# The instructions of a 64-tile attention kernel in new orders on all five engines

## The reference

```python
y   = clip(modulated_linear(x, style) + bias, -256, 256)
q   = l2norm(layernorm(y) @ Wq) * q_scale        # 16 heads of 64
k, v = y @ Wk, y @ Wv ; k = l2norm(k) * k_scale  # 2 null keys in front
x1  = x + softmax(8 * q @ k.T + alibi, causal) @ v @ Wout
kx  = modulated_linear(x1, style2)               # per token: 16 heads of 16
om  = modulated_linear(softmax(kx @ kx.T / 4) @ kx, style3)   # over the heads of one token
gates -> cluster, tile of 64 (argmax twice) ; comp = tanh(gelu(om @ w1) @ w2)
out = x1 + layernorm(om + mag(comp, tables[tile]) * directions[tile])
```

## Time and profile before

| | |
|---|---|
| time, median of 3 runs | 1833.0 us (1832.64 to 1834.09) |
| profiled execution | 1833.11 us |
| its span, first to last instruction | 1831.3 us |
| busy: PE, DVE, ACT, POOL | 94%, 84%, 65%, 64% |
| mean granted clock of PE | 0.97 |
| instructions | 62542 |

### The profile page before, as it was taken

The page is one execution under the profiler, slowest core; times in us unless marked ns, Lnnn a source line. Parts: engine busy times, 40 slices in busy tenths (PEclk is TensorE's granted clock), DMA queues, the critical chain, the costliest instruction groups (busy, mean ns, idle before and its releaser), DMA issues.

```text
span 1831.3 us, 62542 instructions
## 1 busy us (share of the span) xinstructions
PE 1718.0 (94%) x24806; PEld 1439.5 (79%) x24806; DVE 1545.9 (84%) x4182; ACT 1198.5 (65%) x2418; POOL 1173.0 (64%) x903
## 2 busy tenths in 40 slices
PE   4789999999999999999999999999999999999752
PEld 3568888888888888888888888888888888888641
DVE  5567799888989998889989988899899888998744
ACT  2456677777667777776676777676777777667431
POOL 0345557776777677767776777677767776776433
PEclk8899999999999999999999999999999999999875
DMA  4001222222222221222122212221222122212221
GB/s 150 15 9 29 42 49 49 49 55 59 48 46 53 59 49 45 53 59 49 45 56 56 52 42 55 56 52 45 55 54 55 43 52 55 55 47 50 55 54 44
DMA packets 341245, 93.63 MB, mean 51 GB/s; under 512 B 278289, under 2 KB 338097, under 8 KB 341169
## 3 DMA queue, kind: packets, MB, share of 16 engines
q1 hardware_dynamic: 338096, 82.04, 20.6%
q0 software_dynamic: 3072, 10.52, 2.1%
HBM read 58.95 MB, written 33.55 MB: 51 GB/s over the span
## 4 chain that ended last, share of the span: by engine, by line
PE 88%; DVE 5%; ACT 2%; POOL 1%; DMA 1%; issue 1%; SPq 1%; POOLq 0%; ACTq 0%; DVEq 0%
PE pa L442 29%; PE pb L421 7%; PE pa L449 6%; PE ps L645 6%; PE ps L487 6%; PE ps L472 5%; PE ps L479 4%; PE pc L542 4%; PE pc L622 3%; PE pa L421 3%; PE ps L557 3%; PE pb L433 3%; PE ps L489 2%; PE pb L551 2%; PE pb L428 2%; PE pc L568 1%
## 5 line engine op out<-in xcount | busy, mean ns | idle before, releaser
L1131 POOL TENSOR_TENSOR rn<-nrg,mhalf 128x16 f32<-128x16 f32 x64 | 186.6, 2915 | 160.6 <-DVE nrg L1037 160.6
L1117 POOL TENSOR_TENSOR rn<-nrg,mhalf 128x16 f32<-128x16 f32 x64 | 193.2, 3018 | 119.5 <-DVE nrg L970 119.4
L442 PE MATMUL pa<-wv,y 128*128 128x512 f32 x768 | 209.6, 409 | 0.0
L442 PE MATMUL pa<-wq,xnTs 128*128 128x512 f32 x768 | 205.1, 411 | 0.3 <-ACT kcat L703 0.3
L442 PE MATMUL pa<-wk,y 128*128 128x512 f32 x768 | 194.3, 402 | 0.9 <-ACT qn L722 0.9
L442 PEld LDWEIGHTS pa<-wq,xnTs 128*128 128x128 f32 x768 | 139.3, 191 | 51.8 <-issue 23.5
L442 PEld LDWEIGHTS pa<-wk,y 128*128 128x128 f32 x768 | 139.3, 188 | 30.9 <-ACT qn L722 1.7
L1111 POOL TENSOR_TENSOR pr<-pr,rden 128x1056 f32<-128x1056 f32 x64 | 124.7, 1949 | 54.5 <-DVE rden L943 51.8
L442 PEld LDWEIGHTS pa<-wv,y 128*128 128x128 f32 x768 | 135.4, 189 | 23.2
L1006 DVE TENSOR_TENSOR qn<-qn,rn 128x1024 f32<-128x1024 f32 x64 | 112.7, 1762 | 15.6 <-POOL rn L1117 15.0
L1092 POOL TENSOR_TENSOR kn<-kn,rn 128x1024 f32<-128x1024 f32 x64 | 122.0, 1905 | 5.0
(11 more groups left out here) (216 smaller groups left out, 4863.3 us busy)
## 6 DMA issues: line engine op xcount, KB each, us to landing
xT<-in_xT SPq DMA_DIRECT2D x64, 128.0 KB
x<-in_x SPq DMA_DIRECT2D x64, 128.0 KB, 2.1
kxdr<-kxn SPq DMA_DIRECT2D x64, 128.0 KB, 1.7
x1d<-x SPq DMA_DIRECT2D x64, 128.0 KB, 1.8
vm<-kxdr SPq DMA_DIRECT2D x128, 64.0 KB
odr<-o SPq DMA_DIRECT2D x256, 32.0 KB
on<-odr SPq DMA_DIRECT2D x64, 128.0 KB
xb<-x1d SPq DMA_DIRECT2D x64, 128.0 KB, 2.2
```

Source lines behind the costliest of these rows:

```text
L442: last = mm(bank, part(lhs(a_, k)), part(rhs(b_, k)), start=(n == 0), stop=(n == 3 * CK - 1))
L1117: g.tensor_tensor(rn[:, 0, :], nrg[:, 0, :], mhalf[:, :], ALU.pow).then_inc(S("q_rsqrt"), 1)
L1131: g.tensor_tensor(rn[:, 1, :], nrg[:, 1, :], mhalf[:, :], ALU.pow).then_inc(S("k_rsqrt"), 1)
```

## The change

The diff, cut to its core. SP:

```diff
-                if live(i, 6):
-                    sp.dma_start(plain(x1d, t6), x1[:, p, :]).then_inc(D("x1_out", p), 16)
+                if live(i, 5):
+                    wait(sp, "kxn_done", t5)
+                    sp.dma_start(plain(kxdr, t5), kxn[:, :]).then_inc(S("kx_out"), 16)
+                    wait(sp, "kx_out", t5, 16)
+                    for u in range(2):
...
                 if live(i, 11):
-                    wait_dma(sp, "x1_out", t11, 1 - p)
-                    sp.dma_start(xb[:, 1 - p, :], plain(x1d, t11)).then_inc(D("x1_back", 1 - p), 16)
+                    wait(sp, "res_done", t11)
+                    sp.dma_start(plain(out_t, t11), res[:, 1 - p, :]).then_inc(D("out", 1 - p), 16)
...
+                if live(i, 9):
+                    wait_dma(sp, "x1_out", t9, 1 - p)
+                    sp.dma_start(xb[:, 1 - p, :], plain(x1d, t9)).then_inc(D("x1_back", 1 - p), 16)
...
```

PE, DVE and POOL where the prediction speaks of them:

```diff
+                if live(i, 4):
+                    wait(pe, "xm2_done", t4)
+                    linear_T(two(pb, C), wk2, xm2).then_inc(S("kxT_mm"), 1)
...
+                if live(i, 1):
+                    wait(pe, "q1_raw", t1)
+                    project(pa[:, 1, :], lambda a, k: y3f[:, 1 - p, a, k, 0:P],
+                            lambda a, k: wk[:, a, k, 1 * 512:2 * 512])
...
+                if live(i, 3):
+                    wait(dve, "probs", t3)
+                    v.tensor_reduce(den[:, :], heads, AX, ALU.add).then_inc(S("den_done"), 1)
+                    wait(dve, "den_done", t3)
+                    v.reciprocal(rden[:, :], den[:, :]).then_inc(S("rden_done"), 1)
+                if live(i, 7) or live(i, 8):
+                    if live(i, 8):
+                        wait(dve, "local_exp", t8)
+                    route = links_from(0, t7)
                     route(v.tensor_scalar(fl[:, :, :], esc[:, :, :], 1.0, None, ALU.add))
                     route(v.reciprocal(fl[:, :, :], fl[:, :, :]))
                     route(v.scalar_tensor_tensor(out=over[:, :, :], in0=bc(both(fl), 2, KN), scalar=float(KN - 1),
                                                  in1=bc(CO["steps"], 1, 2 * NC), op0=ALU.mult, op1=ALU.subtract))
+                if live(i, 4):
+                    wait(dve, "x1T", t4)
+                    modulate(xm2, two(pb, 0), sty[:, 1, :, :], t4).then_inc(S("xm2_done"), 1)
...
+                if live(i, 3):
+                    wait(pool, "rden_done", t3)
+                    g.tensor_tensor(heads, heads, bc(rden[:, :], 2, J), ALU.mult).then_inc(S("pr_norm"), 1)
...
+                if live(i, 9):
+                    wait_dma(pool, "x1_back", t9, 1 - p)
+                    g.tensor_tensor(xb[:, 1 - p, :], xb[:, 1 - p, :], gb[:, 1, :], ALU.add)
```

More of the change, by code:

```diff
@@ L512, in step @@
[L512 to L536, removed]
+                if live(i, 7):
+                    if 1 - p == 1:
+                        nc.tensor.transpose(pb[:, C:C + P], hidn[:, :, :].rearrange("p u h -> p (u h)"), ident[:, :])\
+                            .then_inc(S("hT_mm"), 2)
@@ L545, in step @@
                     last.then_inc(S("mix_scores"), 1)
[L546 to L553, removed]
-                if live(i, 4):
[L555 to L559, removed]
+                if 1 - p == 1:
+                    if live(i, 7):
+                        wait(pe, "gelu_done", t7)
+                if live(i, 4):
+                    wait(pe, "x1_done", t4)
+                    to_T(two(pb, 0), x1[:, p, :]).then_inc(S("x1T"), 1)
+                if live(i, 2):
+                    wait(pe, "v1_done", t2)
+                    four(pa[:, 1, :], qn, 4).then_inc(S("qT1_mm"), 1)
                 if live(i, 1):
@@ L581, in step @@
+                if live(i, 3):
+                    wait(pe, "pT_done", t3)
+                if live(i, 4):
+                    wait(pe, "kxn_done", t4)
+                if live(i, 6):
+                    wait_dma(pe, "on2_in", t6, p)
+                    to_T(two(pb, 0), on2[:, p, :]).then_inc(S("omT"), 1)
+                if live(i, 3):
                     for r in range(HP):
                         for t, s in ((0, 0), (1, 1), (1, 0), (0, 1)):
-                            last = pv_tile(r, t, s, p)
+                            last = pv_tile(r, t, s, 1 - p)
@@ new lines, in step @@
+                if live(i, 5):
+                    for g in range(QG):
+                        last = fn(kbd[:, g, :], pc[:, 0:2 * P], ACT.Identity, bias=0.0, scale=pick4[:, g:g + 1])
+                    last.then_inc(S("mask_done"), 1)
+                if live(i, 3):
+                    wait(act, "pr_sub", t3)
+                    fn(pr[:, :, :, :], pr[:, :, :, :], ACT.Exp).then_inc(S("probs"), 1)
+                if live(i, 7):
+                    if 1 - p == 1 and live(i, 9):
+                        wait(act, "comp_mm", t9)
+                    if 1 - p == 1:
+                        wait(act, "hT_mm", t7)
+                    if 1 - p == 1:
+                        fn(hT[:, :], pb[:, C:C + P], ACT.Gelu, bias=b1[:, :]).then_inc(S("gelu_done"), 2)
@@ new lines, in step @@
+                if live(i, 7):
+                    if 1 - p == 1:
+                        wait(act, "comp_mm", t7)
+                    if 1 - p == 1:
+                        for o in range(2):
+                            last = fn(comp[:, :, o], pb[:, C + P:C + P + 4].rearrange("p (u o) -> p o u", o=2)[:, o, :], ACT.Tanh,
+                                      bias=b2[:, o:o + 1])
+                        last.then_inc(S("comp_done"), 2)
+                if live(i, 3):
+                    wait(act, "pv_mm", t3)
@@ new lines, in step @@
+                if live(i, 8):
+                    wait(dve, "scores_done", t8)
+                    v.tensor_tensor(own[:, :, :], sc[:, p, :].rearrange("p (c k) -> p c k", k=TPC),
+                                    bc(chosen[:, p, 0, :], 2, TPC), ALU.mult).then_inc(S("own_done"), 1)
+                    wait(dve, "own_done", t8)
+                    v.tensor_reduce(lsc[:, :], own[:, :, :].rearrange("p c k -> p k c"), AX, ALU.add)\
+                        .then_inc(S("local_score"), 1)
+                if live(i, 7):
+                    wait(dve, "zT_mm", t7)
+                    modulate(zd, two(pb, C), dem[:, 2, :, :], t7).then_inc(S("z_dem"), 1)
+                    wait(dve, "z_dem", t7)
+                    v.tensor_tensor(zT[:, :, :], zd[:, :, :, :].rearrange("p k b l -> p k (b l)"),
+                                    bc(cols[:, OB, :], 2, P), ALU.add).then_inc(S("zT_done"), 1)
@@ L895, in step @@
+                if live(i, 3):
+                    wait(dve, "sim_mm", t3)
                     v.tensor_tensor(by_slot(pr)[:, :, 0:R7, :], ps[:, 0:2, 0:R7 * J].rearrange("p t (r j) -> p t r j", j=J),
@@ L1022, in step @@
-                if live(i, 5):
-                    wait(dve, "x1T", t5)
-                    modulate(xm2, two(pb, 0), sty[:, 1, :, :], t5).then_inc(S("xm2_done"), 1)
-                if live(i, 6):
-                    wait(dve, "mix_exp", t6)
-                    v.tensor_reduce(sm2[:, :], A2[:, :, :], AX, ALU.add).then_inc(S("mix_sum"), 1)
-                    wait(dve, "mix_sum", t6)
-                    v.reciprocal(sm2[:, :], sm2[:, :]).then_inc(S("mix_rsum"), 1)
-                    wait(dve, "mix_rsum", t6)
-                    v.tensor_tensor(A2[:, :, :], A2[:, :, :], bc(sm2[:, :], 2, H), ALU.mult).then_inc(S("a_done"), 1)
```

662 lines of the change are left out of this document (315 added, 347 removed).

## The result

| | before | after |
|---|---|---|
| time, median (4 runs each) | 1833.0 us (1832.6 to 1834.1) | 1845.2 us (1844.1 to 1845.4) |
| ratio, 95% interval | | 1.0064 (1.0047 to 1.0082) |
| span of the profiled execution | 1831.3 us | 1842.3 us |
| period, 53 steps (tile 9's q projection to tile 62's) | 26.11 us | 26.90 us |

What follows compares the result with a forecast made beforehand. PE bounded the kernel before (26.08 us a step); after, a PE and DVE loop of 26.4 would. 1833.1 less 34 at the ends plus 17 in steady steps gives 1816 us, range 1797 to 1845.

Steps and rivals of the forecast that it cites:

- The ends: Filling and emptying of the pipeline, tail included: 34 us gained together, bounds 20 and 40.
- The 2.4 us that I added for dropped waits: Fill: followed loss of 19.6 us taken as 22, against 33.5 before, for a gain of 11.5.
- The tail: After the last score matmul to the kernel's end: 28 us, against 30.4 before.
- The gain of the emptying: From step 64 to the end, tail included: loss 63 instead of 86.9 us, gain 24, taken as 22.5.
- my 3 us for dropped waits: Emptying: 3 us added to a followed PE loss of 32, making 35 instead of 62.3.
- the routing block: Steady step: DVE's routing instruction, 0.29 us, held 1.6 beside POOL's pr_norm, in front of xm2.
- The loop: Steady step: PE kx linear to omT, DVE om to rden, routing, xm2; 26.4 us, 0.3 longer than PE's step.
- DVE's term: DVE's part of the steady cycle, from om to rden: 16.6 us.
- the steady term, +17: Steady steps: 0.3 us lost in each of 58 steps, 17 us in all.
- rival 2: Steady step: gamma's hold 0.6 and table load 0.25 also count; a good half real, 0.8 a step, 1845 us; chance 0.28.
- Rival 1: Steady step: no stall, only 0.05 us a step lost; 1802 us (1794 to 1808); chance 0.23.
- rival 3: Ends gain only 20 us and steady steps cost 20; 1833 us; chance 0.07.

Runs made afterwards that it cites:

- run 3: Changed kernel with DVE's routing part 0 to 2 moved behind the copy pn, and yn moved behind the two y-low subtractions: 1807.1 us.
- run 1: Changed kernel with DVE's routing part 0 to 2 moved from in front of xm2 to behind the copy pn: 1808.6 us.
- run 6: Changed kernel, every order kept, with POOL's pr_norm made to wait for the third routing instruction: 1805.2 us.
- run 11: Changed kernel with yn moved behind the two y-low subtractions and ScalarE's Gelu replaced by Identity: 1814.4 us.
- run 2: Changed kernel with yn moved behind the two y-low subtractions, so POOL's gamma multiply cannot get between them: 1824.5 us.
- run 7: Changed kernel with ScalarE's Gelu replaced by Identity, so table loads fall from 67 to 3: 1831.7 us.
- run 4: Changed kernel with POOL's addition of beta moved from the step's end to the next step, in front of gamma: 1847.2 us.
- run 9: Changed kernel with routing behind pn, yn behind the y-low subtractions, and the exp table loaded early on every second step: 1802.7 us.

## Why the prediction was wrong

**The ends were about right.** The first k projection started at 54.39 and took 3.05 (57.4 for 57.9); the kn transposes began at 66.22, for 66.35; steps 2 and 3 of the fill ended at 75.51 and 96.54, for 75.6 and 96.5:

```profile
54.39 3.05 PE L441 MATMUL pa<-wk,y 128*128 128x512 f32 x12
66.22 1.06 PE L448 MATMUL pa<-ident,kn 128*128 128x128 f32 x8 [1.62 <-POOL kn L1123]
75.51 3.16 PE L441 MATMUL pa<-wv,y 128*128 128x512 f32 x12
96.54 1.67 PE L441 MATMUL pa<-wv,y 128*128 128x512 f32 x6
```

The 2.4 us that I added for dropped waits were not there (gain 13.9 for 11.5). The tail behind the last score matmul is 28.1 us (1842.3 less 1814.2) for 28. The gain of the emptying is 5 us less than I took: steps 65, 66 and 67 took 22.9, 21.9 and 17.1, not 20.4, 17.5 and 14.5, and my 3 us for dropped waits cover only a part of that. In 65 and 66 PE waits 1.11 and 2.10 for xm2, because the routing block is in the emptying too, and I had priced it in steady steps alone; in run 3 PE waits 0.51 for it in step 66 (last line):

```profile
1736.97 1.16 PE L420 MATMUL pb<-xm,wk 128*128 128x128 f32 x8 [1.11 <-DVE xm L880]
1758.12 1.16 PE L420 MATMUL pb<-xm,wk 128*128 128x128 f32 x8 [2.10 <-DVE xm L880]
1813.07 1.11 PE L657 MATMUL pb<-wsc,zT 128*128 128x136 f32 x4
1720.13 1.16 PE L420 MATMUL pb<-xm,wk 128*128 128x128 f32 x8 [0.51 <-DVE xm L880]
```

From tile 62's q projection to the end it is 155.3 us in the changed kernel, and 150.6 in run 3; between tile 63's and the end 128.8 and 125.2. How much of that is the block is not shown: in run 1, without the block, the latter is 128.8 too. What else made the three steps longer stays open.

**The loop was the right one**, and its terms can be read off one turn, om 1018.40 to om 1045.20: DVE from om to rden's end 17.14 (forecast 16.6); routing and xm2 2.76 (2.92); kx linear to om 6.90 (6.9). Sum 26.80, 26.98 in the next turn, for 26.4. L988 took 1.83 for 1.9, and run 6 shows its hold as the cause. The 0.5 that is missing is DVE's term: 17.14 holds gamma's 0.53 and the 0.22 for the q squares; without them it is 16.39, 0.2 under my figure. In the next turn the q squares are in time, but res holds L951 (0.59, not 0.18), which I had not named. So my 26.4 is itself too long: 16.39 + 2.76 + 6.90 is 26.05 (an estimate from this one turn), no more than PE's own step. That run 11 comes out at 26.34, and its time at 1814.4, so near to my 1816, is in part luck, since gamma's hold on L909 fills the difference.

**The step that failed** is the steady term, +17: in "I take 26.4 and 58 steps" the loop's DVE part leaves out gamma's hold and the wait for the exp table, which stand in rival 2 alone. The steady steps lost 42.0 us, 26.90 a step. Rival 2 had the same loop with "0.6 + 0.25" on top and "a good half real, 0.8 a step: 1845"; the period rose by 0.79, to the 26.9 that I had named as its sign, and the time is 1845.2. That it meets the time to 0.2 us is luck: its 46 us in the steady steps were 42, and its 34 at the ends 31. Runs 2 and 7 price its terms at 0.34 and 0.23 a step, 0.57 together, and run 11 without them is at 26.34. I had both terms from the rows, in a loop that I had found to be closed already; I gave them to a rival because PE before had absorbed such holds. That argument didn't apply: before, PE was the bound and DVE waited 1.39 a step for it. In the closed loop a hold on DVE's half has no such wait to go into; one beside PE's half has (run 4). Rival 1 (no stall) fell with L988, rival 3 with the ends, which are 31 us shorter than before (they lost 120.4, now 89.0 and a start 0.4 later), not 20.

PE's largest steady wait is for xm2, and qn takes 1.22, as forecast. The q1 wait is there too (2.8 us in 15 times), as the only other one.

## What to carry to other kernels

When a released engine (POOL by rden) and the releasing one go on at the same moment, look at the very next instructions of the releasing engine: put first those that were not held here, which read PSUM (xm2, 0.42 beside pr_norm in run 1) or reduce (L948, 1.21 beside a POOL multiply), or have the other engine wait until the short one is past (run 6, 40 us for one wait). Whether a held instruction costs anything depends on who stands behind it: a hold of 1.14 us behind xm2 brought PE no wait, one of 1.54 in front of it cost 40 us in all. Once a loop over two engines is longer than the bound engine's own step, every hold in it belongs in the sum and none in a rival. Taking one away can give less than its length, when the other engine's instruction then meets the next in line (0.34 of 0.54 in run 2).

## What the hardware showed beyond that

A large POOL multiply (1.96 us) held a DVE tensor_scalar with one SBUF input (1.77) as it did the one with two (1.83); small ones are held as well (L951 0.59 beside res, 0.18 alone). The reductions keep their time, as the prediction said of max and norms; before, of these the maximum alone stood beside a large POOL instruction in the steady state (1.25 beside kn), and after, the k norm does too (1.21 beside L1112). It works the other way too: kn, 1.90 us in its first tile (64.18), takes 2.61 when begun 0.85 before DVE's qn ends, and 2.11 when begun 0.36 before that (qn 1005.06 and 1032.00, 1.22 each). But POOL's powers of 2.9 us on 128x16 did not hold L963: this subtract, with two SBUF inputs of 128x1056 and 128x16, takes 1.25 and ends before the power beside it does (1003.89, beside L1121 at 1002.43). There the rule that the prediction cites from the Trainium skill, that the later one blocks fully, does not fit, and the measurement decides.

```profile
1003.89 1.25 DVE L963 TENSOR_TENSOR pr<-pr,mx 128x1056 f32<-128x1056 f32 x1
1002.43 2.91 POOL L1121 TENSOR_TENSOR rn<-nrg,mhalf 128x16 f32<-128x16 f32 x1
1005.43 2.61 POOL L1123 TENSOR_TENSOR kn<-kn,rn 128x1024 f32<-128x1024 f32 x1
1032.86 2.11 POOL L1123 TENSOR_TENSOR kn<-kn,rn 128x1024 f32<-128x1024 f32 x1
```

What stays open is why run 9's second steps lengthen only from tile 19 or so on; four of its five runs lie at 1801.5 to 1803.7 and one at 1795.9, as if that one had stayed on the short side.
